# Later thresholds for one share of GpSimd's gathers in a mixture-of-experts loop

## The chip, the cores and the metric

The kernel runs on one core of one Trainium2 chip. The metric is the device time of one execution in microseconds (us). All times of the trace count from the start of the profiled execution's span.

## The reference, cut to what matters

The input is 128 sequences of 125 positions with 64 channels. Three layers follow each other:

```python
h = tok(x)                       # depthwise convolution (5 taps, stride 2), norm over the sequence, PReLU -> 128 x 63 x 64
h = h + attn(layernorm(h))       # selective state-space scan over the 63 positions, 16 states a channel
h = h + ffn(layernorm(h))        # mixture of 64 experts, the best 2 of each token

# ffn, for 8064 tokens of 64 channels
logits = xf @ Wr + br
topk_logits, topk_idx = top_k(logits, 2)
gates = softmax(topk_logits)
for e in range(64):
    y = relu(xf @ W1[e] + b1[e]) @ W2[e] + b2[e]        # 64 -> 128 -> 64
    out = out + combine[:, e:e+1] * y                    # combine holds the two gates of a token
```

The change touches the last layer alone.

## The kernel before, in words

The 8064 tokens are 63 positions of 128 rows (one row a partition). They go through the experts in three **shares** of positions: 0 to 15, 16 to 39 and 40 to 62 (`SHARES`). For each share VectorE and TensorE work out a slot for each token and each of its two experts, so that the slots of one expert stand together in tiles of 128 rows.

**Scatters.** GpSimd (POOL) writes the normalised tokens to their slots in a DRAM tensor, `sorted_rows`: one indirect DMA for each position and choice, 126 in all (line 630).

**The loop of rounds.** Two tiles are a pair, two pairs are a step; the shares have 24, 28 and 28 steps, 80 in all, and `STEP0` is [0, 24, 52, 80]. PE, ACT and DVE walk through rounds k = 2 to 83, which are pipelined: in round k PE does the second layer of step k-4 (line 903), the first layer of step k-2 (line 894) and, where k is even and under 80, transposes the rows of the next unit of four pairs (line 885). In rounds 13, 21, ... 69 it also transposes gates (line 910), and ACT copies them in the same rounds (line 1156); in rounds 15, 23, ... 71 it adds biases (line 917). The last of PE's instructions of a round adds 1 to the semaphore `s_pstep`, so that `s_pstep` is k+1 once round k is done. In each round ACT and DVE first wait for `s_pstep` to be k+1; then ACT copies the transposed rows (line 1152, even rounds), applies the activation (line 1161) and starts DMAs: rows of a later unit (line 370) and the store of step k-5's result to `expert_out` (line 1170). DVE does its half of the activation (line 1584) and copies the second layer's result (line 1593). PE's round k waits for ACT's round k-2. SP loads the weights of the experts from DRAM into a ring for 23 pairs (line 439).

**Gathers.** POOL reads the results of a share back with 126 further indirect DMAs into `y1` and `y2`, which lie in the tensor `xt` (line 651). Before the first gather of a share it waits until all stores of that share have landed. Behind the loop DVE multiplies the gathered rows by their gates and adds them (lines 1641 and 1643), and SP writes the output.

**What sets POOL's pace.** Scatters and gathers are numbered d = 0 to 251 in POOL's order: 0 to 125 are the scatters, 126 to 157 the gathers of the first share, 158 to 205 those of the second and 206 to 251 those of the third. Before its DMA, `keep_pace(d)` may wait. The table `STEP_AT` gives, for every second d from 62 to 212, a step; POOL then waits until `s_pstep` is that step plus 4. In the kernel before one straight line serves all of them: the step is (d - 60) * 80 // 153. For the second share's gathers this is 51 at d = 158, 52 at 160, 58 at 172 and 75 at 204.

Of the kernel before, what the change touches and what calls it, by code (L numbers as in the profile page):

```python
# [19 lines left out]
L = 63  # L20
# [23 lines left out]
SHARES = ((0, 16), (16, 40), (40, L))  # L44
# [24 lines left out]
PAIR0, UNIT0, STEP0 = ([sum(v[:h]) for h in range(len(SHARES) + 1)] for v in (PAIRS, UNITS, STEPS))  # L69
# [9 lines left out]
EVERY = 2  # L79
GROUP_AT = {6: 3, 12: 4, 20: 5, 40: 6, 44: 7, 48: 8}  # L80
OFFSETS_AT = {26: 2, 52: 3}
STEP_AT = {d: (d - FIRST_STEP - LAG) * STEP0[-1] // 153 for d in range(FIRST_STEP + LAG + EVERY, FIRST_STEP + LAG + 154, EVERY)}


def slab(n):
# [62 lines left out]
def build(nc, x, w, b, gamma, beta, alpha, A_log, D_param, scale, W_dt, b_dt, W_B, b_B, W_C, b_C,  # L148
# [5 lines left out]
    with ExitStack() as ctx:  # L154
# [304 lines left out]
        def _(pool):  # L459
# [156 lines left out]
            def keep_pace(d):  # L616
# [3 lines left out]
                if d in OFFSETS_AT:  # L620
                    pool.wait_ge(s_off, OFFSETS_AT[d])
                if d in STEP_AT:
                    pool.wait_ge(s_pstep, STEP_AT[d] + LATE)

# [1048 lines left out]
```

## Time and profile before

| | us |
|---|---|
| median of 3 runs | 828.19 |
| the runs | 827.23, 828.19, 837.27 |
| the profiled execution | 836.15 |
| its span | 834.3 |
| rounds of the loop (PE) | about 515 to 762 |
| gathers of the third share (POOL) | 765 to 825 |

The profile is of an execution of its own. Its span is 1.85 us shorter than its time; the rest lies around the span. PE is busy for 58% of the span, DVE for 67%, ACT for 38% and POOL for 72%. These shares average over stages with different limits, and the change touches only a stretch of POOL's work from about 684 us on.

### The profile page before, as it was taken

How to read it: one execution, taken by the hardware profiler on the slowest of the kernel's cores; microseconds unless marked ns; L12 is line 12 of the kernel's file. 1: busy time of each engine (PE TensorE's matmuls, PEld its weight loads, DVE VectorE, ACT ScalarE, POOL GpSimd, SP SyncE). 2: the span in 40 equal slices, each digit the busy share in tenths (PEclk: the TensorE clock that was granted, in tenths of full speed). 3: DMA queues.
4: the chain of work that ended last, by engine and by line, in shares of the span. 5: the costliest groups of instructions: out<-in, count | busy, mean ns of one | idle time of the engine just before them, and what ended most of it. 6: DMA issues, size and time to landing. Idle time of an engine off the chain costs nothing.

```text
span 834.3 us, 8865 instructions
## 1 busy us (share of the span) xinstructions
PE 485.4 (58%) x2514; PEld 314.4 (38%) x2520; DVE 559.4 (67%) x1180; ACT 318.9 (38%) x582; POOL 597.6 (72%) x393
## 2 busy tenths in 40 slices
PE   4735144575557665755764855888777893784000
PEld 3734011222222222222443433766665672673000
DVE  1597799999999999999754735444554561336311
ACT  2159856556646655452340411223322331231000
POOL 5995769999999999995066636566665636663774
PEclk9968569879898779787856666899999996997555
DMA  7999970000000000000045002688988894852211
GB/s 237 382 197 126 85 5 0 0 1 0 0 0 0 0 0 0 0 0 1 1 117 144 22 14 86 176 242 235 255 241 242 244 285 116 234 163 85 74 38 27
DMA packets 106604, 84.95 MB, mean 102 GB/s; under 512 B 30464, under 2 KB 90240, under 8 KB 106560
## 3 DMA queue, kind: packets, MB, share of 16 engines
q1 hardware_dynamic: 79312, 54.76, 30.3%
q10 hardware_dynamic: 19184, 21.40, 8.6%
q0 software_dynamic: 8064, 8.27, 4.0%
q8 instruction: 19, 0.31, 0.2%
q14 instruction: 25, 0.20, 0.1%
HBM read 57.22 MB, written 33.49 MB: 109 GB/s over the span
## 4 chain that ended last, share of the span: by engine, by line
PE 27%; DVE 20%; POOL 19%; issue 16%; ACT 8%; another core or an unknown queue 5%; SPq 1%; ACTq 1%; DMA 0%; POOLq 0%; DVEq 0%
PE ps L903 8%; POOL x_w L578 7%; POOL w_ring L571 6%; PE ps L894 6%; POOL xt L651 5%; DVE hh_ring L1408 4%; PE ps L885 3%; PE ps L676 2%; ACT ps L1057 2%; DVE w_ring L1402 2%; ACT ps L1063 2%; PE ps L740 2%; DVE w_ring L1387 2%; DVE x_w L1584 1%
## 5 line engine op out<-in xcount | busy, mean ns | idle before, releaser
L740 PE MATMUL ps<-x_w,ident 128*128 128x512 f32 x252 | 151.8, 760 | 102.4 <-POOL x_w L578 102.4
L630 POOL DMA_INDIRECT sorted_rows<-xp,slot_i x126 | 122.0, 968 | 106.3 <-issue 32.5
L651 POOL DMA_INDIRECT xt<-expert_out,slot_i x126 | 122.4, 972 | 78.3 <-issue 32.3
L571 POOL TENSOR_TENSOR w_ring<-xt,bc 128x2016 f32<-128x2016 f32 x32 | 143.1, 4472 | 13.5 <-DVE hh_ring L1408 7.3
L1408 DVE TENSOR_TENSOR_SCAN hh_ring<-ps,w_ring 128x1024 f32<-128x1024 f32 x64 | 145.8, 2278 | 0.1
L578 POOL TENSOR_TENSOR x_w<-hh_ring,bc 128x2016 f32<-128x2016 f32 (+1 forms) x32 | 140.7, 4397 | 1.0 <-PE ps L740 1.0
L740 PEld LDWEIGHTS ps<-x_w,ident 128*128 128x128 f32 x252 | 59.2, 245 | 197.7 <-POOL x_w L578 125.7
L1063 ACT ACTIVATE ps<-dt_t,a_exp 128x1024 f32<-128x1024 f32 x64 | 71.5, 1117 | 64.2 <-DVE hh_ring L1408 64.2
L1057 ACT ACTIVATE ps<-dt_t,a_exp 128x1024 f32<-128x1024 f32 x64 | 71.6, 1118 | 52.1 <-DVE w_ring L1387 52.1
L1152 ACT ACTIVATE x_w<-ps 128x512 f32<-128x512 f32 x40 | 23.9, 597 | 145.0 <-remote 50.3
L1387 DVE TENSOR_TENSOR w_ring<-ps,w_ring 128x1008 f32<-128x1008 f32 x64 | 76.7, 1199 | 3.4 <-ACT ps L1057 3.4
L1402 DVE SCALAR_TENSOR_TENSOR w_ring<-ps,w_ring 128x1008 f32<-128x1008 f32 x64 | 75.5, 1180 | 0.0
L1584 DVE TENSOR_SCALAR x_w<-ps,dt_t 128x128 f32<-128x128 f32 x70 | 21.5, 345 | 58.3 <-remote 22.2
L903 PE MATMUL ps<-dt_t,x_w 128*128 128x128 f32 x280 | 43.7, 302 | 22.0 <-DVE x_w L1593 10.8
L1584 DVE TENSOR_SCALAR x_w<-ps,x_w 128x128 f32<-128x128 f32 x56 | 17.3, 345 | 50.8 <-remote 31.4
L903 PEld LDWEIGHTS ps<-dt_t,x_w 128*128 128x128 f32 x280 | 38.2, 210 | 26.3 <-issue 23.2
L903 PE MATMUL ps<-x_w 128*128 128x128 f32 x224 | 34.0, 296 | 20.8 <-issue 16.1
L903 PEld LDWEIGHTS ps<-x_w 128*128 128x128 f32 x224 | 29.6, 205 | 23.7 <-issue 19.7
L1593 DVE COPY x_w<-ps 128x256 f32<-128x256 f32 x80 | 33.1, 414 | 0.9 <-PE ps L903 0.8
L740 PE MATMUL ps<-hh_ring,ident 128*128 128x512 f32 x16 | 11.4, 852 | 33.3 <-ACT hh_ring L1046 26.1
L885 PE MATMUL ps<-ident,x_w 128*128 128x128 f32 x160 | 29.0, 307 | 1.9 <-issue 1.5
L894 PE MATMUL ps<-x_w,dt_t 64*128 64x128 f32 x280 | 28.0, 316 | 0.2 <-issue 0.2
(209 smaller groups left out, 890.1 us busy)
## 6 DMA issues: line engine op xcount, KB each, us to landing
dt_t<-packed SPq DMA_DIRECT2D x140, 96.5 KB
x_w<-packed SPq DMA_DIRECT2D x112, 96.5 KB
x_w<-sorted_rows ACTq DMA_DIRECT2D x40, 256.0 KB
expert_out<-x_w ACTq DMA_DIRECT2D x80, 128.0 KB
sorted_rows<-pad_rows SPq DMA_DIRECT2D x2, 3584.0 KB, 24.2
bc<-packed SPq DMA_DIRECT2D x68, 96.5 KB
packed<-in_L_ffn_W SPq DMA_DIRECT2D x3, 2048.0 KB, 41.9
x_w<-in_x SPq DMA_DIRECT2D x7, 448.0 KB, 9.5
```

Source lines behind the costliest of these rows:

```text
L571: pool.tensor_tensor(w_buf(k, 2), up3[:, bass.ds(c * DC, DC), 1:S].unsqueeze(1).broadcast_to([P, 2, DC, L]), vec_of(k, 2), ALU.mult).then_ ...
L578: pool.tensor_tensor(hc_buf(k, n), h_buf(k, n), vec_of(N + k, n), ALU.mult).then_inc(s_hcp, n)
L630: pool.indirect_dma_start(out=sorted_rows[h], out_offset=bass.IndirectOffsetOnAxis(ap=slot_i[:, c, l:l + 1], axis=0), in_=xn[:, l, :], in_ ...
L651: pool.indirect_dma_start(out=y[:, l, :], out_offset=None, in_=expert_out[h], in_offset=bass.IndirectOffsetOnAxis(ap=slot_i[:, c, l:l + 1] ...
L740: ins = pe.matmul(ps[:, i, :], ident[:, :], src[:, i * BANK:(i + 1) * BANK], start=(k < 0), stop=(k == (N - 2 if last else N - 1)), skip_g ...
L894: last = pe.matmul(ps[:, 2 + 2 * (i % 2) + t, j * P:(j + 1) * P], w_of(n)[t * C:(t + 1) * C, t, 0:HID], xT_e[t * C:(t + 1) * C, i // 2 % 2 ...
L903: last = pe.matmul(ps[:, 6 + i % 2, (2 * j + t) * OUT:(2 * j + t + 1) * OUT], hT_e[:, i % 2, t, j, :], w_of(n)[:, t, HID + C - OUT:HID + C ...
L1057: act.activation(banks(6, 2), d, ACT.Tanh, scale=a_exp[:, 2, k:k + 1]).then_inc(s_th, 1)
L1063: act.activation(banks(2 + 2 * (k % 2), 2), d, ACT.Exp, scale=a_exp[:, 1, k:k + 1]).then_inc(s_dA, 1)
L1387: dve.tensor_tensor(wv, body(banks(6, 2)), wv, ALU.mult).then_inc(s_g, 1)
L1402: dve.scalar_tensor_tensor(out=wv, in0=body(dA), scalar=1.0, in1=wv, op0=ALU.add, op1=ALU.mult).then_inc(s_b, 1)
L1408: dve.tensor_tensor_scan(hh_ring[:, k % 4, :], dA, w_ring[:, k % 4, :], 0.0, ALU.mult, ALU.add).then_inc(s_h, 1)
```

## The change

`STEP_AT` gets new values for the second share's gathers: a line of their own from step 54 at d = 158 to step 80 at d = 206, which is applied to every second d from 160 to 206. Nothing else changes, and no instruction is added, removed or moved: what differs are constants in POOL's waits.

```diff
 STEP_AT = {d: (d - FIRST_STEP - LAG) * STEP0[-1] // 153 for d in range(FIRST_STEP + LAG + EVERY, FIRST_STEP + LAG + 154, EVERY)}
+B_FIRST, B_LAST = 2 * L + 2 * SHARES[1][0], 2 * L + 2 * SHARES[1][1]
+STEP_AT.update({d: STEP0[2] + 2 + (d - B_FIRST) * (STEP0[3] - STEP0[2] - 2) // (B_LAST - B_FIRST)
+                for d in range(B_FIRST + EVERY, B_LAST + 1, EVERY)})
```

With `FIRST_STEP` = 44, `LAG` = 16, `EVERY` = 2, `L` = 63, `B_FIRST` is 158 and `B_LAST` is 206. The value of `s_pstep` that POOL waits for (step + 4), before and after the change:

| d | 158 | 160 | 162 | 164 | 166 | 168 | 172 | 178 | 180 | 182 | 190 | 192 | 198 | 200 | 202 | 204 | 206 |
|---|---|---|---|---|---|---|---|---|---|---|---|---|---|---|---|---|---|
| before | 55 | 56 | 57 | 58 | 59 | 60 | 62 | 65 | 66 | 67 | 71 | 73 | 76 | 77 | 78 | 79 | 80 |
| after | 55 | 59 | 60 | 61 | 62 | 63 | 65 | 68 | 69 | 71 | 75 | 76 | 79 | 80 | 81 | 82 | 84 |

## Rows read from the trace of the kernel before

**Rows 1.** Busy time by stretch: each engine's us (instructions), granted clock, DMA share, GB/s.

```profile
673.00:684.00 11.00, 10.07 (x93) 8.71 (x92) 8.07 (x28) 4.95 (x15) 0.36 (x1) 1.00 0.93 263
684.00:702.70 18.70, 6.22 (x58) 5.22 (x56) 2.65 (x10) 1.26 (x4) 13.30 (x14) 0.78 0.56 162
```

**Rows 2.** Timeline of POOL from 684 us: start, us, instruction, [idle before <- releaser].

```profile
684.15 0.95 POOL L651 DMA_INDIRECT xt<-expert_out,slot_i  x1 [10.79 <-DMA expert_out<-x_w]
...
692.93 0.95 POOL L651 DMA_INDIRECT xt<-expert_out,slot_i  x1 [0.30 <-issue]
...
700.47 0.95 POOL L651 DMA_INDIRECT xt<-expert_out,slot_i  x1 [0.30 <-issue]
702.95 0.95 POOL L651 DMA_INDIRECT xt<-expert_out,slot_i  x1 [1.53 <-remote]
```

**Rows 3.** Timeline of ACT from 678 us, the first instruction of some rounds.

```profile
678.11 0.60 ACT L1152 ACTIVATE x_w<-ps 128x512 f32<-128x512 f32 x1 [1.97 <-PE ps L885]
...
681.97 0.60 ACT L1152 ACTIVATE x_w<-ps 128x512 f32<-128x512 f32 x1 [1.69 <-PE ps L885]
...
683.52 0.37 ACT L1161 ACTIVATE x_w<-ps,bc 128x128 f32<-128x128 f32 x1 [0.44 <-PE ps L894]
...
686.26 0.60 ACT L1152 ACTIVATE x_w<-ps 128x512 f32<-128x512 f32 x1 [2.12 <-PE ps L885]
...
702.72 0.60 ACT L1156 ACTIVATE w_ring<-ps 128x512 f32<-128x512 f32 x1 [15.34 <-remote]
...
707.23 0.60 ACT L1152 ACTIVATE x_w<-ps 128x512 f32<-128x512 f32 x1 [3.40 <-remote]
...
726.57 0.61 ACT L1156 ACTIVATE w_ring<-ps 128x512 f32<-128x512 f32 x1
```

**Rows 4.** Timeline of PE in the same stretch.

```profile
687.27 0.66 PE L910 MATMUL ps<-ident,us_lg 128*128 128x128 f32 x4
...
703.88 2.08 PE L903 MATMUL ps<-x_w 128*128 128x128 f32 x8 [12.16 <-issue]
```

**Rows 5.** Timeline of POOL from 646 us, a group of four gathers and the next.

```profile
646.59 0.95 POOL L651 DMA_INDIRECT xt<-expert_out,slot_i  x1 [1.40 <-PE ps L910]
...
650.36 0.95 POOL L651 DMA_INDIRECT xt<-expert_out,slot_i  x1 [0.30 <-issue]
652.74 0.95 POOL L651 DMA_INDIRECT xt<-expert_out,slot_i  x1 [1.43 <-remote]
```

**Rows 6.** Timeline of ACT beside it.

```profile
646.35 0.60 ACT L1152 ACTIVATE x_w<-ps 128x512 f32<-128x512 f32 x1 [4.49 <-PE ps L910]
...
648.00 0.60 ACT L1156 ACTIVATE w_ring<-ps 128x512 f32<-128x512 f32 x1 [0.53 <-remote]
...
652.51 0.60 ACT L1152 ACTIVATE x_w<-ps 128x512 f32<-128x512 f32 x1 [3.40 <-remote]
```

**Rows 7.** Timeline of POOL at the end: last gathers of the second share, first and last of the third.

```profile
753.64 0.95 POOL L651 DMA_INDIRECT xt<-expert_out,slot_i  x1 [1.76 <-PE ps L894]
754.89 0.95 POOL L651 DMA_INDIRECT xt<-expert_out,slot_i  x1 [0.30 <-issue]
764.97 1.02 POOL L651 DMA_INDIRECT xt<-expert_out,slot_i  x1 [9.13 <-DMA expert_out<-x_w]
...
824.05 0.95 POOL L651 DMA_INDIRECT xt<-expert_out,slot_i  x1 [0.30 <-issue]
```

**Rows 8.** Timelines of ACT in the last rounds and of DVE, its last copy.

```profile
749.02 0.37 ACT L1161 ACTIVATE x_w<-ps,dt_t 128x128 f32<-128x128 f32 x1 [2.60 <-PE ps L894]
...
753.40 0.60 ACT L1152 ACTIVATE x_w<-ps 128x512 f32<-128x512 f32 x1 [3.76 <-PE ps L894]
...
756.82 0.37 ACT L1161 ACTIVATE x_w<-ps,bc 128x128 f32<-128x128 f32 x1 [1.79 <-PE ps L894]
...
759.71 0.37 ACT L1161 ACTIVATE x_w<-ps,bc 128x128 f32<-128x128 f32 x1 [2.26 <-PE ps L894]
...
761.96 0.42 DVE L1593 COPY x_w<-ps 128x256 f32<-128x256 f32 x1 [0.76 <-PE ps L903]
```

**Rows 9.** Timeline of DVE behind the loop, its second wait for a gather.

```profile
787.87 0.69 DVE L1641 TENSOR_TENSOR xt<-xt,gate 128x512 f32<-128x512 f32 x1 [9.27 <-DMA xt<-expert_out,slot_i]
```

**Rows 10.** The gathers' line: durations ns min/median/max, first and last start.

```profile
L651 POOL DMA_INDIRECT xt<-expert_out,slot_i x126: 946/952/1467, 624.6 to 824.1; - x126
```

## The prediction

> **What bounds the kernel now.** I first read the end of the chain of waits. From 764.97 us it consists of POOL's 46 gathers of the third share, back to back until 824.05 [rows 7]: (824.05 - 764.97) / 45 = 1.31 us for each, of which 0.95 us is the instruction and 0.30 us the gap [rows 2, 10]. DVE is ahead of them and waits (9.27 us before one multiplication) [rows 9]. The first of the 46 was released by the last store to `expert_out` [rows 7], which belongs to the last round of the loop. So this kernel ends some 70 us after the last round, whatever the second share's gathers do, as long as they are out of the way by then. The change can move the end only by moving the **last round**.
>
> Next I read the timelines of POOL and ACT side by side, since ACT's first instruction in a round shows when `s_pstep` became visible. Line 1156 runs in rounds 13, 21, ... 61, 69 only, and 726.57 is its last [rows 3]; so 702.72 is round 61, and 686.26, 683.52, 681.97 and 678.11 are rounds 60, 59, 58 and 56. It fits that the gather at 702.95 is the fifteenth of its share, d = 172, which waits for `s_pstep` = 62.
>
> Three paces can be seen:
> - Without gathers (POOL idle for 10.79 us up to 684.15 [rows 2]): rounds 56 to 58 take 681.97 - 678.11 = 3.86 us, **1.93 us a round** [rows 3].
> - With gathers paced by the table: POOL releases four, from 646.59 to 650.36 + 0.95 = 651.31 [rows 5]. ACT starts one round at 646.35, the next at 648.00, while POOL works, and the one after at 652.51, 1.20 us behind the group [rows 6]. So two rounds take 6.16 us, **3.08 us a round**.
> - In the burst: at 684.15 the table lies behind the loop, and fourteen gathers (d = 158 to 171) go out without a stop until 700.47 + 0.95 = 701.42 [rows 2]. Round 60 comes through at 686.26. PE's gate transposes of round 61 stand at 687.27 to 687.93 [rows 4], yet ACT sees the round at 702.72, 1.30 us behind the burst, after an idle time of 15.34 us [rows 3]. PE itself then stands for 12.16 us [rows 4], and the DMAs move 162 GB/s in place of 263 [rows 1].
>
> From the last two I take a rule of this kernel, read off and not explained by the trace: **while POOL sends gathers back to back, about one round comes through, and the next is seen some 1.2 us after the last gather**. The length of a burst is then a delay on the loop, and the loop is on the path.
>
> **The change, part by part.** Instructions and their order stay; only what POOL waits for differs. Adding no instruction costs nothing, and there is nothing of SP's or ACT's queue to be moved.
>
> *1. The burst.* At 684.15 round 59 is visible (683.52), so `s_pstep` is 60. With the new table d = 158 to 163 need at most 60 and pass; d = 164 needs 61, which round 60 gives at 686.26, before POOL gets there; d = 166 needs 62, that is round 61. So the burst has **8 gathers in place of 14**. The eighth starts at 692.93 in the trace and ends at 693.88 [rows 2]; plus 1.2 us, round 61 is seen at 695.1 in place of 702.72: **-7.6 us**. The price is bounded by 0 (the idle time has another cause and stays) and by -12.2, all of PE's idle time [rows 4]. I take -7.6, the rule's value.
>
> *2. The clock.* The stretch of the stall has a granted clock of 0.78 of full speed on average, in place of 1.00 before it [rows 1], and PE's first group of eight matmuls behind it takes 2.08 us [rows 4]. Round 62 then follows 4.5 us behind round 61, at 707.23 [rows 3]. With PE idle for about 3.5 us only, as it is between other groups of gathers, I expect full clock there: two gathers (2.2 us), 0.2 us before and 1.2 us behind make 3.6 us, so **-0.9 us**. Bounds: 0 and -2.6 (a round at 1.93 us).
>
> *3. Rounds 61 to 78.* From round 61 on the new table asks at d = 166, 168, ... 180 for 62, 63, ... 69, exactly what the old one asked at d = 172 to 186. The groups are the same ones with other numbers, and the single place where both lines skip a value moves by a few rounds. I count **0**, with the bounds -1.2 and +1.2, one release of POOL more or less.
>
> *4. The last rounds.* The six gathers held back have to go somewhere. Before, the last two of the share go at 753.64 and 754.89, with round 78 (seen at 753.40), and rounds 79 to 83 are free of them [rows 7, 8]. Now d = 198 waits for 79, so that eight gathers are left when round 78 is seen. Four go as one group with rounds 78 and 79; by the paced case round 80 is seen 6.1 us after round 78, where it now takes 756.82 - 753.40 = 3.42 [rows 8]: +2.7. Two (d = 202, 203) go with round 80; round 81 takes 3.6 us in place of 759.71 - 756.82 = 2.89: +0.7. The last two (d = 204, 205) need 82, round 81; round 82 comes through, and round 83, whose copy by DVE is at 761.96 now, is seen 3.6 us after round 81 in place of 2.25: +1.3. Sum **+4.7 us**. Lower bound 0: rounds 80 to 83 have no row transposes, and round 77, seen at 749.02, came through in the middle of six gathers [rows 8], so the rule may not hold for such rounds. Upper bound +7.5: all six gathers at the full 1.25 us each.
>
> *5. Behind the loop.* The last gather of the second share ends 2.4 us after round 81, about when DVE copies round 83; the last store lands later still (764.97 is 3.0 us behind that copy [rows 7, 8]). So it hides. At d = 206 the new value is 84, which the stores of the last step imply. DVE takes the first share's rows first and waits for the third share's alone [rows 9]. **0 us**; the cover is the last store's 3.0 us, and once it is used up each us counts fully.
>
> Of the gathers' own length, the row has 0.946 to 1.467 us with a median of 0.952 [rows 10]; the long ones can only be a few. The Trainium skill says on this ("SBUF — State Buffer", section "SBUF: two separate sides") that VectorE and GpSimd share a pair of ports, and that a DMA issued from GpSimd waits for its descriptors while a VectorE instruction holds them. By that page the last two gathers, now nearer to DVE's multiplications, might each grow from 0.95 to 1.47 us, and the sum would be 1.0 us worse; the term above goes by the median.
>
> **Sum:** -7.6 - 0.9 + 0 + 4.7 + 0 = **-3.8 us**. On the profiled execution: 836.15 becomes 832.3. That execution is 8 us above the median and close to the slowest run (837.27). I cannot see whether the stall is as long in the runs near 828; I apply the difference to the median, 828.19 - 3.8 = **824.4 us**.
>
> **The rivals.**
> - *The end eats more than the burst gives (slower).* If round 61 is late for another reason than the burst, for instance because PE itself issued slowly, or if the runs without a profile have a short stall only, the gain of terms 1 and 2 is gone and the last rounds' 4.7 us stay: 828.19 + 4.7 = **832.9**. In its favour: the profiled execution is 8 us slower than the median; against it: the same 1.2 to 1.3 us behind the last gather in both the paced and the burst case. It decides once the stall shrinks by less than 4.7 us.
> - *No change.* Gathers take their toll by number and not by burst; the 48 are the same: 14 at 3.08 - 1.93 = 1.15 us for two make 8.1 us against the burst's 14.8 (from 687.93 to 702.72), but what the burst lost SP used to fill its ring of weights, and this comes back later. Then the time is **827 to 829**.
> - *Only the gain.* Rounds 80 to 83 let gathers pass (lower bound of term 4): 828.19 - 8.5 = **819.7**. With the upper bounds of terms 1 and 2 it could be 828.19 - 14.8 = 813.4.
> - *The change does nothing it says.* The stores of share two could land so late that all new thresholds are passed; at 684.15 the loop is at 60 and the new table asks for up to 82, so this is excluded.
>
> **Chances.** Forecast 0.45 (821 to 827); no change 0.22; slower 0.20 (829 to 834); only the gain 0.13. The **range is 819.5 to 833.5**: from the gain without its price to the price without its gain. About 2%, 16.6 us, is what a measurement of this kernel can tell from no change. No case but the extreme bound reaches 16.6 us on either side: faster by over 2% 0.01, within 2% 0.97, slower by over 2% 0.02 (gathers that run beyond the last store, which push the tail of 46 gathers).
>
> **What the profile after would show.** Term 1: eight gathers in a row behind POOL's wait for the stores, then a pause, and ACT's line 1156 of round 61 about 9 us behind round 60 in place of 16.5. Term 2: PE's matmuls behind it near 1.1 us and a granted clock of 1.00. Term 4: the last gather of the share starts near round 81, and rounds 78 to 83 take some 13 us in place of 8.6. Term 5: POOL's next wait still ends with a store. A long idle time of PE at the same place with eight gathers would refute the rule; so would a round seen in the middle of a long group with transposes.

## The result and the profile after

| | before | changed |
|---|---|---|
| median of 20 runs, us | 832.04 | 828.00 |
| lowest and highest | 827.23 to 837.27 | 823.42 to 832.16 |
| the profiled execution, us | 836.15 | 826.82 |
| its span, us | 834.3 | 825.0 |

The ratio is **0.9951**, with the 95% interval 0.9930 to 0.9972: 4.0 us faster, where 3.8 was forecast, inside the range; the interval leaves 1 out, and the gain is far under 2%. The time itself, 828.0, is 3.6 us above the forecast of 824.4, since 17 more runs put the median of before 3.9 us higher; it even lies in the band that the prediction gave to no change (827 to 829). Only against the 20 runs of the kernel before does it show as a gain. The two profiled executions differ by 9.3 us. The one of before is 4.1 us above its median and that of the change 1.2 below, so their difference shows where time went, not how much a median changes.

First the burst. POOL's timeline of the changed kernel answers to [rows 2]; the lines have moved by three, so that 651 is 654.

```profile
681.95 0.95 POOL L654 DMA_INDIRECT xt<-expert_out,slot_i  x1 [10.86 <-DMA expert_out<-x_w]
...
690.75 0.95 POOL L654 DMA_INDIRECT xt<-expert_out,slot_i  x1 [0.30 <-issue]
693.59 0.95 POOL L654 DMA_INDIRECT xt<-expert_out,slot_i  x1 [1.88 <-remote]
```

Eight gathers, as forecast, end at 691.70. ACT's timeline answers to [rows 3]:

```profile
684.00 0.60 ACT L1155 ACTIVATE x_w<-ps 128x512 f32<-128x512 f32 x1 [2.19 <-PE ps L888]
...
693.35 0.60 ACT L1159 ACTIVATE w_ring<-ps 128x512 f32<-128x512 f32 x1 [8.24 <-remote]
...
694.35 0.61 ACT L1155 ACTIVATE x_w<-ps 128x512 f32<-128x512 f32 x1
...
699.79 0.37 ACT L1164 ACTIVATE x_w<-ps,x_w 128x128 f32<-128x128 f32 x1 [4.32 <-PE ps L920]
```

The rows are rounds 60, 61, 62 and 63. Round 61 is seen 9.35 us behind round 60 in place of 16.46. Round 62 follows at once, and round 63 5.4 us later. PE, which answers to [rows 4], stood still for 6.62 us in place of 12.16, but its first group behind that is as slow as before. Here are the rows on both sides of the stand, with ACT's, first of the kernel before and then of the changed one:

```profile
691.34 0.38 PE L885 MATMUL ps<-ident,x_w 128*128 128x128 f32 x2 [1.07 <-issue]
...
703.21 0.62 ACT L1161 ACTIVATE x_w<-ps,x_w 128x128 f32<-128x128 f32 x2
```

```profile
687.05 0.85 PE L888 MATMUL ps<-ident,x_w 128*128 128x128 f32 x4
...
693.85 0.62 ACT L1164 ACTIVATE x_w<-ps,x_w 128x128 f32<-128x128 f32 x2
...
694.52 2.08 PE L906 MATMUL ps<-x_w 128*128 128x128 f32 x8 [6.62 <-ACT x_w L1164]
```

PE's round 63 waits for ACT's round 61. That round ends at 703.83 before and 694.47 with the change, and PE goes on 0.05 us later in both. So PE's stand follows from ACT seeing round 61 late; it is not where the delay begins. By its own records PE had ended round 61 at 687.93 before and at 685.59 with the change, 14.8 and 7.8 us before ACT saw it, and had gone on to end round 62 (691.72 and 687.90). Whether those matmuls ended later than the trace has it (it models their ends) or the count in `s_pstep` came late to ACT, the traces do not tell. "Held" stands for either below.

The busy times by stretch answer to [rows 1]: granted clock and DMA share stand before the last number, which is GB/s.

```profile
682.00:693.30 11.30, 5.87 (x55) 4.75 (x53) 2.39 (x9) 1.12 (x3) 7.58 (x8) 0.86 0.79 237
693.30:740.80 47.50, 38.54 (x308) 33.26 (x308) 19.04 (x62) 15.20 (x44) 29.20 (x31) 0.89 0.69 189
```

The end, which answers to [rows 7, 8], on POOL, ACT and DVE:

```profile
740.20 0.95 POOL L654 DMA_INDIRECT xt<-expert_out,slot_i  x1 [1.61 <-PE ps L888]
...
749.03 0.95 POOL L654 DMA_INDIRECT xt<-expert_out,slot_i  x1 [1.59 <-PE ps L897]
...
752.81 0.98 POOL L654 DMA_INDIRECT xt<-expert_out,slot_i  x1 [0.30 <-issue]
755.24 1.33 POOL L654 DMA_INDIRECT xt<-expert_out,slot_i  x1 [1.45 <-issue]
```

```profile
740.81 0.60 ACT L1155 ACTIVATE x_w<-ps 128x512 f32<-128x512 f32 x1 [0.23 <-remote]
...
748.80 0.37 ACT L1164 ACTIVATE x_w<-ps,bc 128x128 f32<-128x128 f32 x1 [3.70 <-PE ps L897]
```

```profile
751.94 0.42 DVE L1596 COPY x_w<-ps 128x256 f32<-128x256 f32 x1 [0.47 <-PE ps L906]
```

740.81 is round 78, 748.80 round 80, 751.94 DVE's last copy, in round 83. The last gather of the share (752.81) starts 0.87 us behind the start of that copy, and the third share's first one 3.30 us behind it, 3.01 before. With these rows (and round 63 before, seen at 708.71) the 9.3 us divide as follows.

| piece | before | changed | difference |
|---|---|---|---|
| start to round 60 | 686.26 | 684.00 | -2.3 (ahead of the change's place) |
| round 60 to 61 | 16.46 | 9.35 | -7.1 |
| 61 to 63 | 5.99 | 6.44 | +0.4 |
| 63 to 78 | 44.69 | 41.02 | -3.7 |
| 78 to the last copy | 8.56 | 11.13 | +2.6 |
| last copy to the third share's first gather | 3.01 | 3.30 | +0.3 |
| from there to the end | 69.33 | 69.76 | +0.4 |

### The profile page after: what moved, and what is told of

It reads as the page before. It is cut to its first block, busy times and chain, and to the rows that moved or that the text cites. A ratio compares the mean times of both kernels' runs of the same rounds, so it can differ in the third digit from the quotient of the medians.

```text
span 825.0 us, 8871 instructions
## 1 busy us (share of the span) xinstructions
PE 487.8 (59%) x2520; PEld 315.3 (38%) x2520; DVE 559.5 (68%) x1180; ACT 319.5 (39%) x582; POOL 599.0 (73%) x393
## 4 chain that ended last, share of the span: by engine, by line
POOL 31%; PE 29%; issue 16%; DVE 10%; ACT 5%; another core or an unknown queue 5%; SPq 1%; POOLq 0%; ACTq 0%; DMA 0%; DVEq 0%
POOL x_w L581 14%; POOL w_ring L574 10%; PE ps L906 9%; PE ps L897 6%; POOL xt L654 6%; PE ps L888 3%; PE ps L679 2%; PE ps L920 1%; PE ps L828 1%; DVE lstat L1282 1%; PE ps L668 1%; PE ps L770 1%; ACT xp L1096 1%; DVE lstat L1443 1%
## 5 line engine op out<-in xcount | busy, mean ns | idle before, releaser
L1164 ACT ACTIVATE x_w<-ps,dt_t 128x128 f32<-128x128 f32 x70 | 21.7, 371 | 20.1 <-PE ps L888 13.9
```

## The experiments

Theory (**burst theory**): while POOL sends gathers back to back, PE's rounds are held, and the length of a run of gathers is the price. Rivals: the toll goes by the number of gathers, or what helps is the late end. All kernels are the one before with other values in `STEP_AT`, unless the diff says more.

**Two groups of sessions.** Each group of kernels was run together with the kernel before on one chip. Sessions fell into two kinds, by the kernel before itself: 832 to 837 us in some, 752 to 753 us in the others. One and the same chip gave both kinds (832 to 837 in the sessions of e5 and of e6 and e7, 753 in that of e12), so it is no property of a chip. I did not find what decides it. A kernel's ratio is to the kernel before of its own session.

The traces show where the two kinds part. The first scatter is at 417.22 us in the trace of before (832 us kind) and at 416.75 in that of e1 (752 us kind). From there on, while POOL sends its scatters and gathers, the second kind gains: ACT's first copy of rows is at 517.20 and 488.38, its round 60 at 686.26 and 620.02. What matters for the experiments is what POOL does. In all eight traces of the 752 us kind it sends its 126 gathers from some 580 to some 740 us with one pause at most, of 1.27 us at most: it comes to nearly every wait after the loop has passed it. The gathers stood as one long run whatever `STEP_AT` said, and POOL, not the loop, sets the end. So a ratio of 1.000 there says only that the waits had nothing to do. It tests neither the burst theory nor its rivals.

**e1, e8, e11: the burst cut to 8, the end left.**

```diff
+STEP_AT.update({d: 56 + (d - 160) * 19 // 44 for d in range(160, 206, EVERY)})
```

> The kernel before with the burst alone cut: d = 160 to 204 wait for s_pstep 60 to 79, so that 8 gathers go out at once and the last two still go with round 78. Burst theory (rounds are held until a run of gathers ends, the length of the run is the price): round 61 is seen some 9.4 us behind round 60, as in the changed kernel, and the time is at or a little below that of the changed kernel, ratio to before 0.990 to 0.996. Rival (the toll goes by the number of gathers, not by their grouping): ratio 0.998 to 1.002. A third reading (the gain of the change came from the late end): the ratio is clearly nearer to 1 than the 0.9951 of the change.

> The kernel of e1_short_burst_old_end, for a chip on which rounds are held. Burst theory: round 61 some 9.4 us behind round 60 as with the change, ratio to before 0.990 to 0.996, the same as the change within its interval, since in the trace of the change rounds 61 to 83 took 58.6 us with 40 gathers and 59.2 us before with 34: the late end cost nothing in sum. If the gain came from the late end, the ratio is above 0.997. If the late end costs 4.7 us, as predicted, this kernel is at 0.989 to 0.991.

> The kernel of e1 and e8 once more, for a chip on which rounds are held: the burst cut to 8 gathers, the last gathers at their old place. Burst theory: round 61 is seen some 9.4 us behind round 60; ratio to before 0.990 to 0.996, the same as the change within its interval, and the late end of the change cost nothing in sum. If the gain came from the late end, the ratio is above 0.997; if the late end costs the predicted 4.7 us, it is 0.989 to 0.991. On a chip without the hold the ratio is 1.000 within 0.3% for the third time.

e1 and e8 fell into 752 us sessions: 0.9985 (0.9960 to 1.0011) and 1.0004 (0.9978 to 1.0030). e11 fell into one with 836.42 us before: 837.9, ratio **1.0020** (0.9993 to 1.0047). Its ACT shows round 60, round 61, and rounds 66 to 68:

```profile
683.86 0.60 ACT L1153 ACTIVATE x_w<-ps 128x512 f32<-128x512 f32 x1 [1.68 <-issue]
...
694.07 0.60 ACT L1157 ACTIVATE w_ring<-ps 128x512 f32<-128x512 f32 x1 [9.10 <-remote]
...
706.94 0.60 ACT L1153 ACTIVATE x_w<-ps 128x512 f32<-128x512 f32 x1
...
713.92 0.37 ACT L1162 ACTIVATE x_w<-ps,dt_t 128x128 f32<-128x128 f32 x1 [5.87 <-remote]
...
718.39 0.60 ACT L1153 ACTIVATE x_w<-ps 128x512 f32<-128x512 f32 x1 [3.84 <-remote]
```

and POOL beside them, with no pause where a round was seen in time for the next wait:

```profile
706.66 0.95 POOL L652 DMA_INDIRECT xt<-expert_out,slot_i  x1 [1.45 <-remote]
...
715.46 0.95 POOL L652 DMA_INDIRECT xt<-expert_out,slot_i  x1 [0.30 <-issue]
718.63 0.95 POOL L652 DMA_INDIRECT xt<-expert_out,slot_i  x1 [2.22 <-remote]
```

The burst went as expected (10.2 us from round 60 to 61), and yet nothing was gained. The 40 other gathers now go between rounds 61 and 78, and formed runs of 8 and three of 6; DVE's last copy is at 759.66, 65.6 us behind round 61, where it was 59.2 before and 58.6 with the change. So **cutting the burst alone does not pay**, against what I expected (0.990 to 0.996). By the bounds set down beforehand, over 0.997 speaks for the late end.

**e3, e6: no burst, late end.**

```diff
+STEP_AT.update({d: 58 + (d - 160) * 20 // 44 for d in range(160, 206, EVERY)})
```

> All waits follow the loop from its real place: d = 160 waits for s_pstep 62, d = 204 for 82, so that only 2 gathers go at 684 us. Burst theory: round 61 is seen 3 to 5 us behind round 60, another 4 to 5 us are gained over the changed kernel before round 61, of which later rounds give back up to 3: ratio to before 0.985 to 0.993. Rival (number of gathers): ratio as the change has, 0.993 to 0.997, or 1.

> The same kernel as e3_no_burst, for a chip on which rounds are held: d = 160 waits for s_pstep 62, d = 204 for 82, so that only 2 gathers go at 684 us. Burst theory: round 61 is seen 3 to 5 us behind round 60 (16.5 before, 9.4 with the change), and the ratio to before is 0.985 to 0.993, below the 0.9951 of the change. Rival (number of gathers): 0.993 to 1. If PE's matmuls come through at once inside a run of gathers, as on the chip of the first four runs, the ratio is 1.000 within 0.3%.

e3: 1.0001 (0.9972 to 1.0030) in a 752 us session. e6, in one with 837.41 us before: 831.2, ratio **0.9936** (0.9906 to 0.9966). Two gathers go at 684 us, and rounds 60 and 61 are

```profile
686.15 0.60 ACT L1153 ACTIVATE x_w<-ps 128x512 f32<-128x512 f32 x1 [2.27 <-PE ps L886]
...
687.70 0.60 ACT L1157 ACTIVATE w_ring<-ps 128x512 f32<-128x512 f32 x1 [0.43 <-PE ps L911]
```

1.55 us apart. The whole burst is gone, 7.8 us more than with the change, but later rounds give them back (last copy at 755.05, below): its interval overlaps that of the change, and it can't be called better. Round 61 came earlier than expected (3 to 5 us), and the gain was still a little under the expected one (0.985 to 0.993).

**e5: no pace at all.**

```diff
+STEP_AT.update({d: 51 for d in range(160, 206, EVERY)})
```

> The kernel before with all waits of the second share's gathers made void (d = 160 to 204), so that 48 gathers go out back to back, some 60 us. Burst theory, where rounds are held as in the trace of before: one or two rounds come through in 60 us, the rest run behind at 1.9 us each; the last round is 20 to 25 us later than before and the time is 3% over before. On a chip as in the last four runs, where ACT saw each round 0.04 us behind PE's last matmul even inside a run of 20 gathers: no round is held and the time is within 0.5% of before. Rival (number of gathers): within 0.5% on every chip.

834.81 us (three runs) became 861.95 (two), ratio **1.0343** (1.0247 to 1.0439), as the burst theory had it. POOL sends all 48 from 679.41 to 739.58:

```profile
679.41 0.95 POOL L652 DMA_INDIRECT xt<-expert_out,slot_i  x1 [10.68 <-DMA expert_out<-x_w]
...
738.63 0.95 POOL L652 DMA_INDIRECT xt<-expert_out,slot_i  x1 [0.30 <-issue]
789.74 1.02 POOL L652 DMA_INDIRECT xt<-expert_out,slot_i  x1 [50.16 <-DMA expert_out<-x_w]
```

Rounds 60 and 61 are seen at 681.51 and 693.65, in the middle of the run, round 62 only at 739.18:

```profile
693.65 0.60 ACT L1157 ACTIVATE w_ring<-ps 128x512 f32<-128x512 f32 x1 [11.03 <-remote]
...
739.18 0.60 ACT L1153 ACTIVATE x_w<-ps 128x512 f32<-128x512 f32 x1 [44.41 <-remote]
...
739.67 0.62 ACT L1162 ACTIVATE x_w<-ps,x_w 128x128 f32<-128x128 f32 x2
```

PE's timeline shows more than the one before did:

```profile
697.41 0.63 PE L895 MATMUL ps<-x_w,dt_t 64*128 64x128 f32 x2
698.56 0.37 PE L895 MATMUL ps<-x_w,dt_t 64*128 64x128 f32 x1 [0.52 <-issue]
699.98 0.37 PE L895 MATMUL ps<-x_w,dt_t 64*128 64x128 f32 x1 [1.05 <-issue]
...
715.36 0.37 PE L918 MATMUL ps<-b2w,w_ring 128*128 128x128 f32 x1 [2.43 <-issue]
718.16 0.37 PE L918 MATMUL ps<-b2w,w_ring 128*128 128x128 f32 x1 [2.43 <-issue]
740.34 2.08 PE L904 MATMUL ps<-x_w 128*128 128x128 f32 x8 [21.81 <-issue]
```

PE itself slows to one matmul in 1.4 to 2.8 us with nothing recorded to wait for, where a group of eight takes 1.1 us elsewhere. Its last stand, 21.81 us, is again the wait for ACT: ACT's round 62 ends at 740.29, and PE's round 64 starts at 740.34. The number of gathers is unchanged, so the rival by number falls: their grouping costs.

**e7: memsets in the place of gathers.** 46 gathers go behind the loop.

```diff
+STEP_AT.update({d: STEP0[3] for d in range(160, 206, EVERY)})
...
                         for l in range(a, z):
+                            if 2 * L + 2 * a + c * (z - a) + l - a == 160:
+                                for _ in range(28):
+                                    ch.link(pool.memset(pad_rows[:, :], 0.0))
                             keep_pace(2 * L + 2 * a + c * (z - a) + l - a)
```

> Of the second share's gathers two go at 684 us, the other 46 wait for the end of the loop (s_pstep 84); in the place of d = 160, 28 memsets of 128x512 run on POOL back to back, some 16 us, about the length of the old burst. If POOL being busy holds PE's rounds, round 61 is seen some 15 us behind round 60. If only the gathers' DMAs do it, rounds 60 to 83 run at 1.9 to 2.2 us each and the loop ends some 30 us earlier than before, while the tail is 46 x 1.26 = 58 us longer: time about 25 to 35 us over before.

One execution, 857.74 us (the kernel before in the same session: 837.41), 20 us more where 25 to 35 were expected. POOL and then ACT's rounds 60, 62 and 64:

```profile
684.17 16.30 POOL L653 MEMSET pad_rows<- 128x512 f32 x28
```

```profile
684.03 0.60 ACT L1156 ACTIVATE x_w<-ps 128x512 f32<-128x512 f32 x1 [2.27 <-PE ps L889]
...
687.70 0.60 ACT L1156 ACTIVATE x_w<-ps 128x512 f32<-128x512 f32 x1 [1.00 <-PE ps L889]
...
692.45 0.60 ACT L1156 ACTIVATE x_w<-ps 128x512 f32<-128x512 f32 x1 [1.50 <-PE ps L889]
```

No round is held during 16.3 us of a busy POOL: a busy POOL is not enough, and it is the gathers that do it, by their instructions or by their transfers. DVE's last copy is at 728.02, 44.0 us behind round 60, where it was 75.7 before: the gathers cost the loop 31.7 us.

**e4: a run of 20.**

```diff
+STEP_AT.update({d: 51 for d in range(160, 178, EVERY)})
```

> The kernel before with the waits of d = 160 to 176 made void, so that 20 gathers go out at once; from d = 178 the waits are the old ones. Burst theory: round 61 is seen 6 x 1.26 = 7.5 us later than before, some 24 us behind round 60; later rounds have 6 gathers less and give back up to 3.4 us: ratio 1.003 to 1.010. Rival (number): ratio 1.000, and round 61 comes within the run of gathers.

752 us session, ratio 1.0006 (0.9973 to 1.0038), so the run of 20 was not measured where rounds are held. What such a session looks like: here are the first gathers of the second and of the third share, between which POOL makes no pause, then ACT's round 60 and DVE's last copy, and a stretch of 100 us:

```profile
619.85 0.95 POOL L652 DMA_INDIRECT xt<-expert_out,slot_i  x1 [0.30 <-issue]
...
681.38 1.02 POOL L652 DMA_INDIRECT xt<-expert_out,slot_i  x1 [0.30 <-issue]
```

```profile
620.17 0.60 ACT L1153 ACTIVATE x_w<-ps 128x512 f32<-128x512 f32 x1 [2.07 <-PE ps L886]
```

```profile
669.44 0.43 DVE L1594 COPY x_w<-ps 128x256 f32<-128x256 f32 x1 [0.75 <-PE ps L904]
```

```profile
500.00:600.00 100.00, 95.59 (x886) 83.92 (x886) 70.64 (x241) 42.08 (x120) 75.89 (x80) 1.00 1.01 304
```

Beside the scatters and gathers of that stretch PE is busy for 95.6 of 100 us and the DMAs move 304 GB/s (before, in a session with the hold: 241 GB/s from 540 to 660 us). The 48 gathers of the second share form one run, as in e5, and the loop takes 49.3 us from round 60 to the last copy where e5 took 105.2.

**e2, e9, e12: the late end alone.**

```diff
+STEP_AT.update({d: 54 + (d - 158) * 26 // 48 for d in range(192, 206, EVERY)})
```

> The kernel before with the late end alone: d = 192 to 204 wait for 76 to 82, all earlier waits as before, so the 14 gathers still go at once. Burst theory: the stall before round 61 stays at 15 to 17 us behind round 60; the last rounds 78 to 83 take 2 to 5 us longer, and the rounds 71 to 75, free of gathers now, give about as much back: ratio 0.998 to 1.005. If the late end were what helped, the ratio would be 0.995 or less.

> The kernel of e2_old_burst_late_end, for a chip on which rounds are held. Burst theory: round 61 stays 15 to 17 us behind round 60; what the late end moves is given and taken within the loop, ratio 0.998 to 1.004. If the late end were what helped, 0.995 or less.

> The kernel of e2 and e9 once more, for a chip on which rounds are held; with it the four combinations of burst (14 or 8) and end (old or late) are there. Burst theory as first held (only the burst pays): 0.998 to 1.004. What e11 (burst cut, old end: ratio 1.002) and the trace of the change point to (gathers beside rounds 80 to 83 cost no time, and gathers put between rounds 61 and 78 cost what the burst gives): the late end alone gives 3 to 4 us, ratio 0.994 to 0.998, with round 61 still 15 to 17 us behind round 60 and rounds 78 to 83 at no more than 9.5 us. If only both parts together help, 0.999 or more.

All three fell into 752 us sessions: 0.9997, 1.0002 and 1.0000, each within 0.3%. So the fourth combination is **not measured** where it would matter.

**e10: no burst, old end.**

```diff
+STEP_AT.update({d: 58 + (d - 160) * 17 // 44 for d in range(160, 206, EVERY)})
```

> No burst (d = 160 waits for 62) and the last gathers at the old place (d = 204 waits for 79): 48 gathers over rounds 60 to 78 instead of 60 to 81. Burst theory: round 61 some 2 us behind round 60; groups become a little longer, so the gain is that of e6_no_burst_again or smaller, ratio 0.990 to 0.996. If a late end costs, it is better than 0.990.

752 us session: 1.0015 (0.9982 to 1.0048), which says nothing of the hold.

**The sessions with the hold together.** One profiled execution each, from round 60 to DVE's last copy. The kernel before alone spreads over 10 us from run to run, so differences of a few us between these rows show where time lies and not how medians differ:

| kernel | ratio | runs of gathers | us |
|---|---|---|---|
| e7 | | none (2 and memsets) | 44.0 |
| changed | 0.9951 | 8, 4, 4, 4, 4, 2, 2, 4, 6, 6, 4 | 67.9 |
| e6 | 0.9936 | 2, 6, 4, 4, 4, 4, 8, 4, 2, 6, 4 | 68.9 |
| before | 1 | 14, 2, 4, 4, 4, 4, 2, 2, 4, 6, 2 | 75.7 |
| e11 | 1.0020 | 8, 4, 4, 8, 4, 2, 6, 6, 6 | 75.8 |
| e5 | 1.0343 | 48 | 105.2 |

The change and e6 have the same runs in another order (one of 8, two of 6, six of 4, two of 2) and take the same time within 1 us. So the cost goes by how gathers are grouped and not by their number: over e7's 44.0 us, the 48 gathers cost 24 to 25 us in the runs of 2 to 8 of the change and e6, 32 in the groupings of before and of e11, and 61 in one run. I have no formula for it.

Where a run stands matters at the very end. With the change, the last four gathers (from 749.03) lie beside PE's rounds 82 and 83. Here are PE's matmuls of these two rounds, with the change and then in e7, without any gather:

```profile
749.88 2.02 PE L906 MATMUL ps<-bc,x_w 128*128 128x128 f32 x16 [2.04 <-DVE x_w L1596]
```

```profile
725.65 2.33 PE L907 MATMUL ps<-bc,x_w 128*128 128x128 f32 x16
```

They are no slower beside the gathers. From round 80 to the last copy it takes 751.94 - 748.80 = 3.1 us with the change (rounds 80 and 81 are seen together), 4.1 in e6, which has four gathers there too, and 4.0 in e7, where round 80 is seen at 724.03. Gathers there cost next to nothing.

## Why the prediction came out, and which of its steps failed

- *The bound.* Right: the gathers of the third share and what follows moved with the last round, within 0.7 us.
- *What a term measured* is read from one profiled execution of each kernel, 9.3 us apart where the medians are 4.0 apart.
- *Term 1, the burst (-7.6).* Right in size, 8 gathers and -7.1 us. The rule behind it (one round comes through, the next is seen 1.2 us after the run) is only roughly right, and two of the signs that were named against it came. PE stood for 6.6 us with eight gathers, where 3.5 was expected. And rounds with transposes were seen in the middle of long runs: round 61 in e5, 14 us into the run, and round 76 with the change, in the middle of six gathers (731.35 to 738.58):

```profile
731.35 0.95 POOL L654 DMA_INDIRECT xt<-expert_out,slot_i  x1 [1.24 <-PE ps L897]
```

```profile
735.63 0.60 ACT L1155 ACTIVATE x_w<-ps 128x512 f32<-128x512 f32 x1 [2.88 <-PE ps L888]
```

In e5 PE also slowed step by step. For a first run of 8 or 14 right behind a free stretch the rule gave the size.
- *Term 2, the clock (-0.9).* **This step failed.** PE's idle time was 6.6 us, not 3.5, as PE had already done round 62 when it stopped, and its clock fell all the same: the granted clock is 0.50 from 694.52 to 699.55, the lower of the two levels, and the group takes 2.08 us as before. Round 62 was seen 1.0 us behind round 61 in place of 4.5, and round 63 5.4 us behind that in place of 1.5: no gain in sum. Why round 62 was seen at once, when before it was seen only at 707.23, stays open: in both traces PE's record has it done before ACT saw round 61.
- *Term 3, rounds 61 to 78 (0).* **This step failed too**, though the sum did not show it: these rounds, round 62 with them, took 50.7 us before and 47.5 with the change, 3.2 less, where the bound was 1.2. The groups did come out as the same ones with other numbers: runs of 4, 4, 4, 4, 2, 2, 4 and 6 follow each other in both, and to the start of the next run they take 46.2 us before (707.46 to 753.64) and 46.6 with the change (693.59 to 740.20). What the count missed is the run of two ahead of them before, from 702.95; it held the loop for 4.5 us, until the next run began:

```profile
707.46 0.95 POOL L651 DMA_INDIRECT xt<-expert_out,slot_i  x1 [2.31 <-remote]
```

With the change there is no such run: round 62 is seen right behind round 61, so the next wait (d = 168) is passed in time and the first run is one of four. Rounds seen close together merge runs, and that can also go wrong: in e11 rounds 65 and 66 are seen at 706.42 and 706.94, a run of eight goes with them, and from round 61 on e11 takes 6.4 us more than before. How much of the 6.4 is due to which run was not separated.
- *Term 4, the last rounds (+4.7).* Mis-sized: +2.6 in the trace, and the last four gathers cost next to nothing. The price was taken from groups beside rounds with row transposes; rounds 80 and 81 have none, and 82 and 83 have only half of what is left. For those four gathers the lower bound that I gave, 0, was the better value.
- *Term 5, behind the loop (0).* Nearly: +0.7 us, 0.3 of it ahead of the first gather and 0.4 in the tail. The two last gathers of the share took 0.95 and 0.98 us, so the lengthening to 1.47 that the prediction allowed for did not fall on them.
- *The sum.* From round 60 on the changed kernel's profiled execution is 7.0 us shorter, where 3.8 was forecast. Term 1 promised 0.5 more than came; terms 2 to 4 together said 3.8 us longer where it was 0.7 shorter; term 5 left out a cost of 0.7. The medians differ by 4.0 only. That the forecast of 3.8 meets 4.0 is in part luck.
- *The rivals.* "By the number of gathers" is refuted by e5. "A late end eats the gain" did not happen; a cut burst without a late end (e11) is what gave no gain. That the late end alone would pay is argued from the trace and not shown. The caution that a session might have no stall was apt in a way I did not foresee: in 752 us sessions none of five kernels, timed in eight runs, moved the time by more than 0.2%, since there the waits hardly ever stop POOL. The changed kernel itself was not run in one.

## What to carry to other kernels

Waits that only set a pace should be judged by what they make of the groupings over the whole stretch: taking a burst away moves its work elsewhere, and whether that pays depends on the place having slack. Put such work beside rounds that have little of their own, and compare the time from a fixed point before to a fixed point behind, not the stall alone. And run the baseline again in each session: here it moved by 10% between sessions, and in the other kind the waits that the change moves had nothing to do. There the gathers themselves set the end, so first see which of the two, the loop or POOL's queue, ends last.

## What was not expected of the hardware

- In some sessions, runs of POOL's indirect DMAs slowed PE: with 48 in a row one matmul in 1.4 to 2.8 us, rounds seen up to some 50 us late. In others, also on the same chip, hardly anything of it is there: round 60 of e4 is seen 0.03 us behind PE's last matmul (620.14), in the middle of 126 gathers without a pause, and the same kernel takes 752 us in place of 832 to 837. POOL's memsets (16.3 us) do not do it.
- The Trainium skill ("SBUF — State Buffer", section "SBUF: two separate sides") has GpSimd's descriptor writing shut out while VectorE holds the pair of ports that the two share, and says that on the engines' side of SBUF PE never waits on anyone. The first gathers beside DVE's multiplications behind the loop do take 1.02 to 1.33 us in place of 0.95. But the slowed matmuls of e5 are PE's, and a lock between DVE and GpSimd alone does not explain them. The cause stays open; every timed run here recorded its clock and span, so whether recording plays a part is not known.
